# A graph network on one core: the adjacency build on four sets of one-hots, norms with ACT's squares, column sums by DVE, late self loops, and a store in chunks

## The chip, the cores and the metric

The kernel runs on one core of a Trainium2 chip. The metric is device microseconds (us) of one execution. The kernel before was run three times: the median is 2507.62 us, the runs lie between 2501.81 and 2509.18 us.

## What is computed

The reference is a chain of four pre-norm residual layers on a graph of N = 3125 nodes with D = 64 features and E = 103,125 directed edges (50,000 drawn pairs in both directions and one self loop per node), sorted by their target:

```python
h = relu(layernorm(x)); x = x + sage_sum_twice(h)      # L0: agg @ Wl.T + b + h @ Wr.T, row norm between
h = relu(layernorm(x)); x = x + relational(h)          # L1: each edge's message uses one of 16 matrices
h = relu(layernorm(x)); x = x + gat_three_times(h)     # L2: attention over the edges of each target
h = relu(layernorm(x)); x = x + sage_mean_twice(h)     # L3: as below
# sage_mean: agg / max(deg, 1) @ W_neigh.T + h @ W_self.T + b
# after each: leaky_relu((z - mean) * rsqrt(var + eps) * gamma + beta), mean and var over all nodes
```

## The kernel before

**Tiles.** The nodes lie in NT = 25 tiles of P = 125 partitions. The activations (x_sb, l_h, l_z) are 125 x 25 x 64 in fp32, 1600 values a partition. A chunk is TC = 5 tiles, 320 values a partition; there are NC = 5 chunks. The adjacency matrix `adj` lies in SBUF in 16 bits, 25 blocks of 125 rows by 3125 columns and a little padding.

**The build** (L260 to L362) makes `adj` from the edge list. The sorted edges are taken in GB = 202 groups of 512, that is four tiles (GT) of 128 edges. The targets of one group fall in a window of W = 20 columns that starts at a base column, read from `base_row` into a register. For each of the four tiles, DVE writes a one-hot matrix of 500 columns, `col_hot` (L285: block of the source times place in the window). The one-hots of the sources inside a block, `src_hot`, are made by DVE (L288) and by ACT, which makes one or two of the four (`ACT_TILES`) by a square (L306) and a relu (L312). PE multiplies the pairs into a PSUM bank (L349), then adds the window's old content to the same bank by a matmul with the identity (L354), since windows of neighbouring groups overlap; ACT writes the bank back to `adj` (L320). There are two sets of one-hots, two PSUM banks, and each engine's loop has two groups in its body. The waits between the engines are those in this piece of PE's code:

```python
base = pe.value_load(base_row[0:1, bass.ds(g, 1)], min_val=0, max_val=N)   # L344
pe.wait_ge(s_hot, g + 1)        # DVE's one-hots
pe.wait_ge(s_src, g + 1)        # ACT's relus
for t in range(GT): last = pe.matmul(sums, src_hot[...], col_hot[...], ...)  # L349
last.then_inc(s_used, 1)        # DVE may write this set again
pe.wait_ge(s_written, g)        # ACT has written window g - 1
pe.matmul(sums, ident16[...], adj[:, :, bass.ds(base, W)], ...)              # L354
```

The program's loops (`Fori`) are real loops of the chip's sequencers, with a branch at the end of each round; L360 is that of PE's loop. DVE waits for `s_used` of two groups ago.

**Norms.** `layer_norm_relu` runs three times, ahead of l0, l1 and l3, each in a block of its own; it is a chain of whole-width DVE instructions (L400 to L408) with one square root on ACT (L413). The third one, ahead of the last stage, also has POOL subtract the identity from the 25 diagonal blocks of `adj` (L393), which removes the self loops that the attention layers needed. Each block ends in a barrier of all engines.

**Aggregation layers.** `sage_layer` splits h into a high and a low fp16 part (`l_parts`), and PE works chunk by chunk: 50 matmuls of the aggregation (`spmm`, L495), five transposes (L503), then the projections of the chunk before (L514, L515), which DVE reads out of PSUM and turns into z (L451 to L453). In the two layers of the last stage (l3a, l3b), `sums_over_nodes` (L524) adds five fp32 matmuls a chunk with a matrix of ones, which sum z over the nodes.

**Batch norms.** `batch_norm_lrelu` puts the mean together from these sums (L1070 to L1072), subtracts it from all of z (L1073), squares it in five pieces (L1076), sums the squares over the nodes with 25 fp32 matmuls (L1052), and scales, shifts and applies the leaky relu in three DVE instructions of 1600 (L1098 to L1100). After the first of them a bound of h is formed as well. After the second follow `add_residual` (L1624) and `store` (L1633, one DMA of all of x), each in a block of its own.

## Time and profile before

| | |
|---|---|
| median of three runs (lowest to highest) | 2507.62 us (2501.81 to 2509.18) |
| the profiled execution's own time | 2511.9 us |
| its span in the profile | 2509.8 us |
| busy PE, PE's weight loads, DVE, ACT, POOL | 1892.3, 980.2, 1640.6, 1242.8, 1119.8 us |

Busy times are sums over the whole span. By stage, PE's and DVE's shares differ much: the build takes the stretch from 42.5 to 398.4 us, the first layer goes on to 555, the relational layer takes 555 to 1480, the attention layers 1480 to 2289, the last stage the rest. In the rows below PE is TensorE, PEld its weight loads, DVE VectorE, ACT ScalarE, POOL GpSimd, SP SyncE; a q behind an engine marks its sequencer. Each fp32 matmul leaves two records. PEclk is the granted clock of PE as a share of the upper level.

### The profile page before, as it was taken

What the parts mean: (1) busy time and instruction counts of PE and PEld (TensorE: products, weight loads), DVE (VectorE), ACT (ScalarE), POOL (GpSimd) and SP (SyncE); (2) the same over time, 40 slices, a digit from 0 to 9 for tenths busy, and PEclk for the clock granted to TensorE, in tenths of its full rate; (3) what the DMA queues carried; (4) which work ended last, traced back from release to release, by engine and by line L of the source; (5) the groups of instructions that cost most, each with busy time, mean ns of one, the idle gap of its engine ahead of it and who ended that gap; (6) DMA issues with size and microseconds to landing.
All of it is one profiled execution on the core that took longest, in us unless ns stands there. A gap on an engine that the chain in (4) does not pass through costs nothing. (4 is left out here: it accounts for less than half of the span.)

```text
span 2509.8 us, 35723 instructions
## 1 busy us (share of the span) xinstructions
PE 1892.3 (75%) x8956; PEld 980.2 (39%) x8957; DVE 1640.6 (65%) x4139; ACT 1242.8 (50%) x2362; POOL 1119.8 (45%) x1003
## 2 busy tenths in 40 slices
PE   2777776863788878887888865779878876886885
PEld 1333333541344434443443445234423342332654
DVE  8888885223565655665665635998699869984222
ACT  5777773111333333333333320789578957894010
POOL 3000000006666666666666641578467846785000
PEclk9999998876889889898988975899789979998776
DMA  1000001001111111111111112000000000000000
GB/s 61 0 0 0 0 0 63 1 26 36 35 27 30 31 28 32 28 28 32 28 31 29 28 20 88 1 1 1 1 1 0 1 1 1 1 1 13 1 1 13
DMA packets 28313, 44.95 MB, mean 18 GB/s; under 512 B 12381, under 2 KB 12762, under 8 KB 28115
## 3 DMA queue, kind: packets, MB, share of 16 engines
q0 software_dynamic: 17664, 18.12, 4.5%
q1 hardware_dynamic: 10576, 25.91, 2.8%
q8 instruction: 39, 0.64, 0.1%
q14 instruction: 34, 0.28, 0.0%
HBM read 36.60 MB, written 7.39 MB: 18 GB/s over the span
## 5 line engine op out<-in xcount | busy, mean ns | idle before, releaser
L729 POOL DMA_INDIRECT adj<-h_table,l_idx x544 | 561.2, 1032 | 330.4 <-issue 145.8
L919 DVE TENSOR_SCALAR adj<-adj,node_key 125x1024 f16<-125x1024 f16 x825 | 375.5, 498 | 369.0 <-remote 165.7
L1428 POOL TENSOR_TENSOR gat_ring<-gat_ring,adj 125x750 f32<-125x750 f32 (+2 forms) x375 | 503.3, 1342 | 215.3 <-ACT gat_ring L1484 211.0
L864 PE MATMUL psum<-adj,x_sb 125*128 125x512 f16 x1650 | 447.2, 418 | 57.4 <-DVE adj L919 49.2
L792 ACT ACTIVATE l_z<-psum 128x320 f32<-128x320 f32 x204 | 89.3, 438 | 573.9 <-remote 265.3
L1322 DVE SCALAR_TENSOR_TENSOR gat_ring<-x_sb,gat_node,psum 125x750 f32<-125x750 f32 (+2 forms) x375 | 322.0, 867 | 53.1 <-PE psum L1560 41.7
L1482 ACT ACTIVATE gat_ring<-gat_ring,gat_node 125x750 f32<-125x750 f32 (+2 forms) x375 | 304.4, 812 | 63.7 <-DVE gat_ring L1322 60.1
L1557 PE MATMUL psum<-gat_ring,gat_hx 125*65 125x500 f32 (+1 forms) x500 | 253.4, 599 | 68.5 <-POOL gat_ring L1428 67.7
L349 PE MATMUL psum<-col_hot,src_hot 128*125 128x500 bf16 x808 | 209.6, 381 | 113.1 <-ACT src_hot L312 70.3
L1484 ACT ACTIVATE gat_ring<-gat_ring 125x750 f32<-125x750 f32 (+2 forms) x375 | 271.9, 725 | 11.9
L864 PEld LDWEIGHTS psum<-adj,x_sb 125*128 125x128 f16 x1650 | 169.9, 106 | 262.1 <-DVE adj L919 67.7
L285 DVE TENSOR_SCALAR col_hot<-iota_h,c_tab 128x500 bf16<-128x500 f16 x808 | 227.5, 347 | 53.9 <-PE psum L349 53.8
L1291 DVE SCALAR_TENSOR_TENSOR psum<-adj,gat_node,psum 125x750 f32<-125x750 f16 (+1 forms) x276 | 259.8, 941 | 1.3
L676 POOL IOTA l_z<- 128x320 int32 x1 | 0.4, 393 | 545.1 <-issue 545.1
L495 PE MATMUL psum<-adj,l_parts 125*128 125x500 f16 x1000 | 156.7, 322 | 52.3 <-DVE l_parts L442 52.3
L843 PE MATMUL psum<-adj 128*128 128x320 bf16 x816 | 150.1, 307 | 46.8 <-DMA adj<-h_table,l_idx 44.0
L349 PEld LDWEIGHTS psum<-col_hot,src_hot 128*125 128x125 bf16 x808 | 94.9, 137 | 200.6 <-DVE src_hot L288 141.5
L853 PE MATMUL psum<-l_z,l_rel 128*64 128x120 f32 x1088 | 163.1, 286 | 0.0
L1557 PE MATMUL psum<-gat_ring,gat_o 125*65 125x500 f32 (+1 forms) x250 | 129.8, 614 | 31.8 <-POOL gat_ring L1428 31.4
L853 PEld LDWEIGHTS psum<-l_z,l_rel 128*64 128x64 f32 x1088 | 116.2, 143 | 91.9 <-issue 89.5
L907 DVE TENSOR_SCALAR adj<-l_iota,adj 128x320 bf16<-128x320 f16 x612 | 149.4, 299 | 2.6 <-PE psum L843 2.1
L320 ACT ACTIVATE adj<-psum 125x500 f32 x202 | 123.1, 609 | 51.5 <-PE psum L354 46.1
(241 smaller groups left out, 2205.1 us busy)
## 6 DMA issues: line engine op xcount, KB each, us to landing
adj<-h_table,l_idx POOLq DMA_INDIRECT x544
adj<-key_table SPq DMA_DIRECT2D x33, 250.0 KB
adj_saved<-adj SPq DMA_DIRECT2D x1, 3840.3 KB
adj<-adj_saved SPq DMA_DIRECT2D x5, 768.1 KB
x_saved<-x_sb SPq DMA_DIRECT2D x2, 781.2 KB
x_sb<-x_saved SPq DMA_DIRECT2D x2, 781.2 KB
x_sb<-in_x SPq DMA_DIRECT2D x1, 781.2 KB
out<-x_sb SPq DMA_DIRECT2D x1, 781.2 KB
```

The costliest lines, as they stand in the source:

```text
L285: last = v.tensor_scalar(col_hot[:, half, t, :], iota_h[:, :], c_tab[:, bass.ds(g * GT + t, 1)], None, ALU.is_equal)
L349: last = pe.matmul(sums, src_hot[:, half, t, 0:P], col_hot[:, half, t, :], start=(t == 0), stop=False)
L729: pool.indirect_dma_start(out=to[:, t, :], out_offset=None, in_=table[:, :], in_offset=bass.IndirectOffsetOnAxis(ap=index[:, t:t + 1], axi ...
L853: last = pe.matmul(psum[0:D, SUMS[half], 0:SIX * W], rel[:, r, :], zs[:, half, r, :, :].rearrange("p a w -> p (a w)"), start=(r == 0), sto ...
L864: last = pe.matmul(psum[:, 3 + t, :], h_parts[:, k, :], select[0:P, k % SELECTS, t * GE:(t + 1) * GE], start=(k == 0), stop=(k == NT - 1), ...
L919: v.tensor_scalar(select[0:P, k % SELECTS, :], keys, node_key[:, k:k + 1], None, ALU.is_equal).then_inc(s_sel, 1)
L1291: v.scalar_tensor_tensor(to, here, a_unit[:, k:k + 1], so_far, ALU.min, ALU.max).then_inc(s["max_step"], 1)
L1322: v.scalar_tensor_tensor(by_tile(ring[:, n % RING, 0:width(c)]), by_tile(rrow[:, 0:width(c)]), k_s[:, k:k + 1], in_psum(ROW1, c), ALU.add, ...
L1428: pool.tensor_tensor(slot, slot, adj[:, k, cols(c)], ALU.mult).then_inc(s["weight_ready"], 1)
L1482: act.activation(slot, slot, ACT.Relu, scale=-1.0, bias=neg_a_s[:, k:k + 1]).then_inc(s["exponent_bounded"], 1)
L1484: act.activation(slot, slot, ACT.Exp, scale=-1.0).then_inc(s["exp_ready"], 1)
L1557: last = pe.matmul(sums[:, 0:near, 0:P], hx[:, k, :], by_tile(ring[:, n % RING, 0:near * P]), start=(k == 0), stop=(k == NT - 1))
```

## The change

The change touches six places.

1. The build has four sets of one-hots, four PSUM banks and four groups a round, with a remainder of two groups behind the loop. The weights of its matmuls are 128 columns wide instead of 125. ACT writes the window of three groups ago (`AHEAD`), where it was two, and loads that base behind the squares of its step. The table `cv` of the preparation shares the memory of the new sets.
2. The semaphores of the preparation are cleared by SP while the adjacency's tail is spilled, so that their numbers can be used again.
3. In `layer_norm_relu`, the subtraction and the sum go in five chunks, and ACT makes the squares.
4. Of the 25 self loops, POOL removes 15 in the norm and ten inside the next aggregation layer, ahead of the chunks that read them.
5. z's column sums are taken on DVE: a reduce over the five tiles of a chunk. One accumulating set of five matmuls then sums over the partitions and chunks, for the mean; the squares (now ACT's) are reduced and summed in the same way.
6. The last batch norm scales, shifts and applies the relu chunk by chunk; POOL adds each chunk to x, and SP stores it.

```diff
-ACT_TILES = (2, 1)
+ACT_TILES = (2, 1, 2, 1)
+SETS = len(ACT_TILES)
...
+LATE_LOOPS = 10
...
-        src_hot = sb("src_hot", [128, 2, GT, 128], BF16, build_scope)
-        col_hot = sb("col_hot", [128, 2, GT, W * NT], BF16, build_scope)
...
+        src_hot = sb("src_hot", [128, SETS, GT, 128], BF16, build_scope)
+        col_hot = sb("col_hot", [128, SETS, GT, W * NT], BF16, build_scope)
+        cv = col_hot[:, 2:4, :, :].rearrange("p s t w -> p (s t w)").bitcast(FP32)[:, 0:2 * G * GT]\
+            .rearrange("p (k c) -> p k c", k=2)
...
-                    with dve.Fori(1, GB // 2) as i:
-                        for half in range(2):
-                            dve.wait_ge(s_used, 2 * i + half - 1)
-                            one_hots(2 * i + half, half)
+                    for g in range(SETS):
+                        one_hots(g, g)
+                    with dve.Fori(1, GB // SETS) as i:
+                        for at in range(SETS):
+                            dve.wait_ge(s_used, SETS * i + at - SETS + 1)
+                            one_hots(SETS * i + at, at)
...
+                    def step(g, at):
+                        squares(g, at)
+                        base = base_of(g - AHEAD)
+                        write_columns(g - AHEAD, (at - AHEAD) % SETS, base)
+                        act.wait_ge(s_used, g - SETS + 1)
+                        relus(g, at)
...
-                            g = 2 * i + half
-                            base = base_of(g - 2)
-                            act.wait_ge(s_src, g - 1)
-                            one_hots(g, half)
-                            write_window(g - 2, half, base)
-                            relus(g, half)
...
-                        sums = psum[0:P, half, 0:W * NT]
+                        sums = psum[:, at, 0:W * NT]
                         for t in range(GT):
-                            last = pe.matmul(sums, src_hot[:, half, t, 0:P], col_hot[:, half, t, :], start=(t == 0),
-                                             stop=False)
+                            last = pe.matmul(sums, src_hot[:, at, t, :], col_hot[:, at, t, :], start=(t == 0), stop=False)
...
-                    with pe.Fori(1, GB // 2) as i:
-                        group(2 * i, 0)
-                        group(2 * i + 1, 1)
+                    for g in range(SETS):
+                        group(g, g, g == 0)
+                    with pe.Fori(1, GB // SETS) as i:
+                        for at in range(SETS):
+                            group(SETS * i + at, at)
...
-                        with pool.Fori(0, NT) as t:
...
-                            pool.tensor_tensor(own, own, ident[0:P, 0:P], loops).then_inc(s_loops, 1)
...
+                            pool.tensor_tensor(own, own, ident[0:P, 0:P], ALU.subtract).then_inc(s_loops, 1)
...
-                    link(v.tensor_tensor(tmp, x_sb[:, :, :], over_features(stat[:, 0, :]), ALU.subtract))
-                    link(v.tensor_tensor(h, tmp, tmp, ALU.mult))
-                    link(v.tensor_reduce(stat[:, 1, :], h, AX.X, ALU.add))
+                    for tiles in chunks:
+                        v.tensor_tensor(tmp[:, tiles, :], x_sb[:, tiles, :], over_features(stat[:, 0, tiles], TC), ALU.subtract)\
+                            .then_inc(s_centred, 1)
+                    for c, tiles in enumerate(chunks):
+                        dve.wait_ge(s_squared, c + 1)
+                        link(v.tensor_reduce(stat[:, 1, tiles], h[:, tiles, :], AX.X, ALU.add))
...
+                    for c, tiles in enumerate(chunks):
+                        act.wait_ge(s_centred, c + 1)
+                        act.activation(h[:, tiles, :], tmp[:, tiles, :], ACT.Square).then_inc(s_squared, 1)
...
+                        for t in range(NT - loops, NT):
+                            own = adj[:, t, t * P:(t + 1) * P]
+                            pool.tensor_tensor(own, own, ident[0:P, 0:P], ALU.subtract).then_inc(s_less, 1)
...
+                        if column_sums is not None:
+                            dve.wait_ge(s_zc, c + 1)
+                            v.tensor_reduce(column_sums[:, c, :], zc.rearrange("p t d -> p d t"), AX.X, ALU.add).then_inc(s_sums, 1)
...
+                        if loops is not None and (c + 1) * TC > NT - loops:
+                            pe.wait_ge(s_less, (c + 1) * TC - (NT - loops))
...
-                    def sums_over_nodes(c):
-                        pe.wait_ge(s_zc, c + 1)
-                        bank, place = (5, c) if c < 3 else (4, c - 3)
-                        at = TC * D + place * D
-                        for t in range(TC):
-                            pe.matmul(psum[0:P, bank, at:at + D], ones[0:P, 0:P], z[:, c * TC + t, :], start=(t == 0),
-                                      stop=(t == TC - 1))
...
-                        if c >= 2 and column_sums:
-                            sums_over_nodes(c - 2)
...
+                for done in (s_sg, s_key, s_keys, s_nodes, s_dg, s_ti, s_x, s_mats, s_mats2, s_vecs, s_zeroed, s_zeroed2, s_iota,
+                             s_ident, s_ident2, s_chain, s_diag, s_basebc, s_span, s_spanall):
+                    sp.sem_clear(done)
...
-                        for t in range(NT):
-                            if t % TC == 0:
-                                pe.wait_ge(s_sq, t // TC + 1)
-                            last = pe.matmul(psum[0:P, 1, 0:D], ones[0:P, 0:P], h[:, t, :], start=(t == 0), stop=(t == NT - 1))
-                        last.then_inc(s_sumsq, 1)
...
+                        def over_nodes(bank, parts_of, ready, done):
+                            for c in range(NC):
+                                if ready is not None:
+                                    pe.wait_ge(ready, c + 1)
+                                end = pe.matmul(psum[0:P, bank, 0:D], ones[0:P, 0:P], parts_of[:, c, :], start=(c == 0),
+                                                stop=(c == NC - 1))
+                            end.then_inc(done, 1)
+
+                        over_nodes(5, sums, None, s_mean)
+                        over_nodes(1, square_sums, s_sq, s_sumsq)
...
+                        for c, tiles in enumerate(chunks):
+                            act.wait_ge(s_centred, c + 1)
+                            act.activation(h[:, tiles, :], z[:, tiles, :], ACT.Square).then_inc(s_squared, 1)
...
+                        def _(pool):
+                            for c, tiles in enumerate(chunks):
+                                pool.wait_ge(s_final, c + 1)
+                                pool.tensor_tensor(x_sb[:, tiles, :], x_sb[:, tiles, :], h[:, tiles, :], ALU.add).then_inc(s_added, 1)
+
+                        @block.sync
+                        def _(sp):
+                            for c, tiles in enumerate(chunks):
+                                sp.wait_ge(s_added, c + 1)
+                                sp.dma_start(out[:, tiles, :], x_sb[:, tiles, :]).then_inc(s_out[c], 16)
+                            for c in range(NC):
+                                sp.wait_ge(s_out[c], 16)
...
-                        link(v.scalar_tensor_tensor(bn[:, 0, :], bn[:, 1, :], 1.0 / N, bn[:, 0, :], ALU.mult, ALU.add))
-                        link(v.tensor_tensor(z[:, :, :], z[:, :, :], over_tiles(bn[:, 0, :]), ALU.subtract))
-                        for c in range(NC):
-                            tiles = slice(c * TC, (c + 1) * TC)
-                            v.tensor_tensor(h[:, tiles, :], z[:, tiles, :], z[:, tiles, :], ALU.mult).then_inc(s_sq, 1)
...
+                        link(v.tensor_scalar(bn[:, 0, :], psum[0:P, 5, 0:D], 1.0 / N, None, ALU.mult))
+                        for tiles in chunks:
+                            v.tensor_tensor(z[:, tiles, :], z[:, tiles, :], over_tiles(bn[:, 0, :], TC), ALU.subtract)\
+                                .then_inc(s_centred, 1)
+                        for c, tiles in enumerate(chunks):
+                            dve.wait_ge(s_squared, c + 1)
+                            v.tensor_reduce(square_sums[:, c, :], h[:, tiles, :].rearrange("p t d -> p d t"), AX.X, ALU.add)\
+                                .then_inc(s_sq, 1)
...
+                        else:
+                            for c, tiles in enumerate(chunks):
+                                zc = z[:, tiles, :]
+                                v.tensor_tensor(zc, zc, over_tiles(bn[:, 0, :], TC), ALU.mult).then_inc(s_scaled, 1)
+                                dve.wait_ge(s_scaled, c + 1)
+                                v.tensor_tensor(zc, zc, over_tiles(beta, TC), ALU.add).then_inc(s_moved, 1)
+                                dve.wait_ge(s_moved, c + 1)
+                                v.scalar_tensor_tensor(h[:, tiles, :], zc, 0.01, zc, ALU.mult, ALU.max).then_inc(s_final, 1)
...
-            layer_norm_relu("l3", h[:, :, :], z[:, :, :], ALU.subtract)
...
+                       mat("S_self1"), True, column_sums=sums, loops=LATE_LOOPS)
...
-            add_residual(nc, sem("l3_residual"), x_sb, h)
-        store(nc, sem, out, x_sb)
```

On PE, in the body of the build's loop, one group stands like this before, with the branch behind it (the first of the two groups of a round has no branch):

```order
L344 ISA
L344 TENSOR_LOAD base_row
L344 ISA x2
L345 REGISTER_ALU
L349 MATMUL psum<-col_hot,src_hot 125x500 [waits src_hots_ready,col_hots_ready]
L349 MATMUL psum<-col_hot,src_hot 125x500 x3
L354 ISA [waits window_written]
L354 MATMUL psum<-adj,ident 125x500
L360 REGISTER_ALU
L360 COMPARE_AND_BRANCH
```

And so it stands in the changed kernel, where three more groups of the same form are ahead of it in the round:

```order
L358 ISA
L358 TENSOR_LOAD base_row
L358 ISA x2
L359 REGISTER_ALU
L363 MATMUL psum<-col_hot,src_hot 128x500 [waits src_hots_ready,col_hots_ready]
L363 MATMUL psum<-col_hot,src_hot 128x500 x3
L367 ISA [waits window_written]
L367 MATMUL psum<-adj,ident 128x500
L373 REGISTER_ALU
L373 COMPARE_AND_BRANCH
```

The order within a group is the same; the branch comes once in four groups instead of once in two, and the output has 128 partitions.

On ACT, one step of the build's loop (the one with a single square) reads like this before, from the load of the base to the relu:

```order
L316 ISA
L316 TENSOR_LOAD base_row
L316 ISA x2
L306 ISA [waits src_hots_ready]
L306 ACTIVATE square<-iota_h,lo_tab 128x128
L320 ISA [waits outer_done]
L320 ACTIVATE adj<-psum 125x25x20
L311 REGISTER_ALU
L312 ACTIVATE src_hot<-square 128x128 [waits squares_ready]
```

The same step in the changed kernel:

```order
L315 ISA
L315 ACTIVATE square<-iota_h,lo_tab 128x128
L325 ISA
L325 TENSOR_LOAD base_row
L325 ISA x2
L328 REGISTER_ALU
L329 ISA [waits outer_done]
L329 ACTIVATE adj<-psum 125x25x20
L320 REGISTER_ALU [waits hots_used]
L321 ACTIVATE src_hot<-square 128x128 [waits squares_ready]
```

The base's load has moved from ahead of the square to between the square and the window's write, and the relu now waits for PE's use of its set.

On DVE, the end of the program before, from the scaling of the second batch norm on (the barriers between blocks show as branches; names of semaphores behind a program's middle are those of numbers used before):

```order
L1098 TENSOR_TENSOR l_z<-l_z,l_bn 125x1600 [waits l1_gathered2]
L1099 TENSOR_TENSOR l_z<-l_z,vecs 125x1600 [waits l1_gathered2]
L1100 SCALAR_TENSOR_TENSOR l_h<-l_z 125x1600 [waits l1_gathered2]
L1046 UNCONDITIONAL_BRANCH [waits l1_gathered2]
L1622 UNCONDITIONAL_BRANCH [waits barrier_Pool_Activation_PE_DVE_SP_release]
L1624 TENSOR_TENSOR x_sb<-x_sb,l_h 125x1600
```

In the changed kernel, the first chunk and the start of the second:

```order
L1166 TENSOR_TENSOR l_z<-l_z,l_bn 125x320 [waits src_groups_in]
L1168 TENSOR_TENSOR l_z<-l_z,vecs 125x320 [waits l1_picked_turned]
L1170 SCALAR_TENSOR_TENSOR l_h<-l_z 125x320 [waits l1_picked_T_copied]
L1166 TENSOR_TENSOR l_z<-l_z,l_bn 125x320
L1168 TENSOR_TENSOR l_z<-l_z,vecs 125x320 [waits l1_picked_turned]
```

The three wide instructions have become fifteen narrow ones, and the residual add has left DVE.

## Rows read from the trace of the kernel before

**Rows 1.** Windows by stage: the build. Stretch, length, busy (count), PEclk, DMA share, GB/s.

```profile
42.50:398.40 355.90, 259.90 (x1010) 122.37 (x1010) 299.43 (x1308) 273.73 (x700) 0.00 (x0) 1.00 0.00 0
```

**Rows 2.** Timeline inside the build: start, busy us, engine, line, operation, tiles [idle before].

```profile
199.79 0.63 ACT L320 ACTIVATE adj<-psum 125x500 f32 x1 [0.36 <-PE psum L354]
202.23 0.69 ACT L306 ACTIVATE square<-iota_h,lo_tab 128x128 f16<-128x128 f16 x2 [0.35 <-ACT src_hot L312]
203.36 0.63 ACT L320 ACTIVATE adj<-psum 125x500 f32 x1 [0.43 <-PE psum L354]
201.95 1.03 PE L349 MATMUL psum<-col_hot,src_hot 128*125 128x500 bf16 x4 [0.97 <-ACT src_hot L312]
202.82 0.41 PE L354 MATMUL psum<-adj,ident 125*125 x1
203.07 1.01 PE L349 MATMUL psum<-col_hot,src_hot 128*125 128x500 bf16 x4
200.60 0.41 DVE L288 TENSOR_SCALAR src_hot<-iota_neg,lo_tab 128x128 bf16<-128x128 f16 x2
```

**Rows 3.** PE's sequencer at its loop's end: ns min/median/max, first and last start.

```profile
L360 PEldq FUSED_REGOPS  x100: 59/59/64, 45.9 to 394.1; - x100
L360 PEldq COMPARE_BRANCH  x100: 79/211/234, 49.7 to 397.3; - x100
```

**Rows 4.** Groups of instructions, weight loads: busy, mean ns, idle before, releasers.

```profile
L349 PEld LDWEIGHTS psum<-col_hot,src_hot 128*125 128x125 bf16 x808 | 94.9, 137 | 200.6 <-DVE src_hot L288 141.5 <-issue 28.9
...
L843 PEld LDWEIGHTS psum<-adj 128*128 128x128 f16 x816 | 64.4, 99 | 99.3 <-DVE adj L907 44.0 <-issue 38.4
```

**Rows 5.** Timeline of the first norm, its first and last step shown.

```profile
402.96 1.83 DVE L402 TENSOR_TENSOR l_z<-x_sb,stat 125x1600 f32<-125x1600 f32 x1
...
408.53 0.18 DVE L405 TENSOR_SCALAR stat<-stat 125x25 f32<-125x25 f32 x1
```

**Rows 6.** Timeline of the third norm: POOL's self loops and DVE's subtraction.

```profile
2289.43 14.16 POOL L393 TENSOR_TENSOR adj<-adj,ident 125x125 f32 x25 [7.68 <-PEq L375]
...
2291.43 1.97 DVE L402 TENSOR_TENSOR l_z<-x_sb,stat 125x1600 f32<-125x1600 f32 x1
```

**Rows 7.** PE in layer l3a, timeline; the last row is a window's clock.

```profile
2325.66 6.91 PE L495 MATMUL psum<-adj,l_parts 125*128 125x500 f16 x50
...
2332.93 1.21 PE L524 MATMUL psum<-l_z,ones 125*125 125x64 f32 x10
2333.97 0.38 PE L514 MATMUL psum<-mats,l_agg 128*125 128x64 f32 x2
...
2337.53 8.53 PE L495 MATMUL psum<-adj,l_parts 125*128 125x500 f16 x50
...
2366.23 2.36 PE L524 MATMUL psum<-l_z,ones 125*125 125x64 f32 x10 [1.63 <-DVE l_z L453]
...
2337.40:2340.90 3.50, 3.50 (x15) 0.51 0.00 0
```

**Rows 8.** Groups of POOL's instructions by form, in the attention layers.

```profile
L1428 POOL TENSOR_TENSOR gat_ring<-gat_ring,adj 125x375 f32<-125x375 f32 x75 | 65.8, 878 | 108.3 <-ACT gat_ring L1484 107.5
```

**Rows 9.** Timeline of the second batch norm and the end of the program.

```profile
2474.23 0.49 DVE L453 TENSOR_TENSOR l_z<-l_z,vecs 125x320 f32<-125x320 f32 x1
...
2480.50 2.10 DVE L1076 TENSOR_TENSOR l_h<-l_z 125x320 f32<-125x320 f32 x5
2481.04 10.76 PE L1052 MATMUL psum<-l_h,ones 125*125 125x64 f32 x50 [3.91 <-DVE l_h L1076]
...
2493.24 1.82 DVE L1098 TENSOR_TENSOR l_z<-l_z,l_bn 125x1600 f32<-125x1600 f32 x1
...
2499.32 1.82 DVE L1624 TENSOR_TENSOR x_sb<-x_sb,l_h 125x1600 f32<-125x1600 f32 x1 [0.54 <-PEq L1046]
...
2501.62 0.27 SPq L1633 DMA_DIRECT2D out<-x_sb  x1
```

**Rows 10.** DMA over 2480 to 2512 us, in 40 slices of 0.75 us.

```profile
GB/s 0 0 0 0 0 0 0 0 0 0 0 0 0 0 0 0 0 0 0 0 0 0 0 0 0 0 0 16 96 112 136 120 136 128 128 128 0 0 0 0
```

More of the change, by code:

```diff
@@ L342, in _, with group @@
                 def _(pe):
-                    def group(g, half, first=False):
+                    def group(g, at, first=False):
                         base = pe.value_load(base_row[0:1, bass.ds(g, 1)], min_val=0, max_val=N)
@@ L553, in _ @@
                 act.wait_ge(s_wscale, 3)
+        prep_sems.close()
         with ExitStack() as scope:
```

146 lines of the change are left out of this document (81 added, 65 removed).

## Prediction

> **What bounds the kernel now.** I read the table by stage first. The build of the adjacency blocks takes 356 of 2510 us, at the upper clock level (granted clock 1.00), and no engine in it is full: DVE 299, ACT 274, PE 260 us [rows 1]. Then I read a few groups of it in order of time, and asked which wait ends last. A group is four one-hot matmuls, an identity matmul that adds the old window, and ACT's write of the window. The list of waits names DVE's one-hots as what PE waits for. The times deny it: DVE's one-hots for the matmuls at 201.95 were done at 201.01 (200.60 + 0.41). What ends last is PE's own sequencer. A write ends at 200.42 (199.79 + 0.63); only then does PE issue the identity matmul behind it, take the loop's branch, load the next base, and start the next four matmuls at 201.95. Their identity matmul runs at 202.82, its write from 203.36 to 203.99, and the circle of two groups closes: 1.53 + 0.87 + 0.54 + 0.63 = 3.57 us [rows 2]. The whole build gives 355.9 / 101 pairs = 3.52 [rows 1]. So DVE's idle time is a result of this circle, and its sets of one-hots are not what it runs out of.
>
> The rest that the edit touches is the last 220 us and the norms. The norms are a DVE chain [rows 5]. The two batch norms are bound by PE: 25 fp32 matmuls on single tiles, 10.76 us (50 records, each matmul leaves two) at the lower level [rows 9]. The last stage ends with DVE, a residual add, and one store that is issued at 2501.62 and waited for until 2509.8 [rows 9].
>
> **Build: four sets.** A write still releases the next identity matmul, and the base is still loaded behind it, so the circle stays. What shrinks is the number of branches: 100 become 49. Without a branch, PE goes from one group's matmuls to the next's in 203.07 − 201.95 = 1.12 us; with one, the way from the write's end is 1.53, or 0.41 more at most. The branch's instructions alone take 0.211 + 0.059 us and a third small one [rows 3], so at least 0.27. I take 0.36, between the two, since gaps lie between sequencer instructions too: 51 x 0.36 = **18.5 us** (14 to 21). ACT now writes group g−3 behind its squares. ACT is busy 274 / 202 = 1.36 us a group [rows 1], and in the step with two squares (0.69 [rows 2]) a write, its relu and they come to some 1.5; the circle asks for a write each 1.6 on average, so the order costs nothing, or a few us. If ACT lost 0.1 us a group, 20 us would be gone.
>
> Weights of 128 columns instead of 125 load in 99 ns and not 137 [rows 4]. Only the first load of a group's four is bare on the circle, so 101 x 0.04 = 4 us at most, nothing at least; I take 1, as the matmuls of rows 2 already start within the load. The Trainium skill ("TensorE: Matmul & The Clock Gate", Weight-path perf modes) says that fast weight load is on when the weights are 128 and not fp32, and calls it about twice as fast as measured; the trace agrees in sign, with a factor of 1.4. A factor of two would make the term 7 us at most.
>
> Next to the spill DMA, SP clears twenty semaphores. No row of mine has a clear; at a sequencer instruction's 0.06 us [rows 3] that is 1.2 us, behind ACT's work there by half: **−0.8** (0 to −1.5).
>
> **Norms.** Subtract, square and reduce take 5.57 us as three DVE instructions, 402.96 to 408.53 [rows 5]. Now five subtracts at a spacing of 0.40 (five 320-wide ones take 2.10 [rows 9]) are followed by five linked reduces of 0.49 [rows 9] with 0.03 between them (5.57 less three of 1.83 leaves 0.08): 2.0 + 2.7 = 4.7. ACT's squares lie under them: its write of 500 values takes at most 0.63 [rows 2], so five of 320 end by 3.7 and the last reduce starts later. **0.87** each in two norms. The third is longer than its DVE work, because POOL removes 25 self loops, 14.16 us from 2289.43 on [rows 6], and the next stage waits for it until 2303.6. With 15 there, both end near 2299.5: **4.1** (3 to 5). The ten late ones are needed by the fourth chunk, 40 us on; they may hold DVE's first split by 0.3. Sum of this part **5.5**.
>
> **Column sums off PE.** In each of the two last aggregation layers PE has five sums of five fp32 matmuls. Three lie in its full stream at 1.04 to 1.21 us each, the fourth at the lower clock, 2.36 [rows 7]; DVE's reduce that replaces each is 0.49 and lies in DVE's idle time. 3 x 1.08 + 2.1 = 5.3 a layer, **10.6** for both. (The fifth stands in the next part.)
>
> The clock adds to it. After the stretch of fp32 matmuls 2332.93 to 2337.5 the granted clock is 0.51, that is 1.2 GHz, and the next 50 aggregation matmuls take 8.53 us and not the 6.91 of the chunk before, which followed a shorter such stretch [rows 7]. I give back two such drops of the four: 2 x 1.6 = **3.3** (0 to 6.5).
>
> **Batch norms.** I count from the end of the last z. Before, in the second: squares from 5.78 on, their matmuls end at 17.1, the scaling starts at 18.5 [rows 9]. After: reduce 0.52, barrier 0.54, five matmuls 2.36, a small instruction 0.3 (0.18 [rows 5] and the hand-over): subtract from 3.75 on (so the fifth sum's 2.36 is paid as before); five subtracts to 5.85; five reduces at 0.40 to 7.95; one last matmul 0.7 (2.36 / 5 and the hand-over); then the 1.44 from 2491.80 to 2493.24 as before: scaling at 10.1. **8.4**. The first one also forms a bound, in small DVE instructions that 10 us of matmuls covered; with half a microsecond of them bare now, **7.9** (7 to 8.4).
>
> **Last stage's end.** Before, from 2493.24 to 2509.8: 16.5 us [rows 9]. After, DVE does three linked instructions of 0.49 + 0.03 a chunk, the third followed at a spacing of 0.42 by the next chunk's first: 5 x 1.46, 7.4 to the end of the last. POOL's add of a chunk (878 ns for 375 wide [rows 8], so 0.78 for 320) meets DVE. In the trace, DVE's two-input subtract beside POOL takes 1.97 instead of 1.83 [rows 5, 6], and POOL's loops of 125 values average 0.57 us where 375 values cost 0.88. I charge DVE 0.6 for each of four adds, 2.4 (0 to 3.1). Then the last add 0.85, and a store of a fifth of the bytes: of the whole one's 8.2 us, bytes move in nine slices of 0.75, some 6.6 [rows 9, 10], so 1.6 + 6.6 / 5 = 2.9; I take 3.5, as small rows may move slower. Sum 7.4 + 2.4 + 0.85 + 3.5 = 14.2: **2.3** (0 to 4.7).
>
> The Trainium skill ("GPSIMD Engine Reference", Specifications) says that POOL shares its SBUF interfaces with DVE, with contention where DVE has two SBUF inputs; every instruction of DVE's there has. By this rule the adds would give nothing, the worst end of my range, and the trace's 1.97 beside 1.83 agrees in kind.
>
> **Sum.** 18.5 + 1 − 0.8 + 5.5 + 10.6 + 3.3 + 8.4 + 7.9 + 2.3 = 56.7 us. The profiled execution took 2511.9 (span 2509.8 and 2.1 around it), which gives 2455; the median of the runs is 4.3 lower, so I forecast **2451 us**.
>
> **Rivals.**
> 1. *DVE becomes the build's bound* (0.08). If the waits on used one-hots were the cause, four sets would bring the build to DVE's 299 us of work or a little under, a gain of 57 or more instead of 19: 2451 − 38 = 2413. For it: DVE's share of 84% and its wait on PE. Against it: the circle above, which holds with any number of sets, at 3.57 − 0.36 = 3.2 us a pair.
> 2. *The build gains nothing* (0.12): ACT's new order (two squares and a base load ahead of each write) delays writes by the 0.1 us a group. Then 2451 + 19 = 2470.
> 3. *The clock drops stay, and POOL's adds starve or stall DVE* (0.10): 3.3 and 2.3 are lost: 2457. The rule above, alone, costs 2.3: 2453.
> 4. *Slower* (0.02): ACT's steps serialise. The other stages gain 37 us, so the build must lose 37 + 7.5, that is 0.22 us a group over 202 groups, from 1.76 to 1.98. ACT's work is 274 / 202 = 1.36 us a group [rows 1]; only if a base load of some 0.6 us stood bare in each step, behind the squares' end, would it reach that. At 2.1 us a group it gives 2451 + 19 + 69 = 2539. For it: ACT's write is now the instruction behind the load. Against: the load runs on the sequencer while the squares run on the engine, and the edit puts it there.
>
> **How the numbers follow.** My sum has 0.68, the rivals 0.32. Its own range, by the bounds: build 14 to 25, clock 0 to 6.5, end 0 to 4.7, loops 3 to 5, so 2442 to 2462; some us more for how the unchanged stages fall (the runs shown spread over 7 us). Leaving out rivals 1 and 4 and reaching to most of 2: **2438 to 2469**. A measurement of this kernel tells no change from 0.3%, 7.5 us. Faster 0.97, within it 0.01, slower 0.02.
>
> **What would show it.** Build: the pair of groups at 3.3 us on average, writes in two alternating distances, DVE's idle before its first one-hot of a group smaller but not gone; at 2.9 us rival 1 is right, at 3.5 rival 2. The weight loads of the build at 99 ns. Norms: 4.7 us from the first subtract to the variance. Third norm: next stage 4 us sooner. Aggregation layers: no fp32 sums between chunks, 50-matmul chunks at 6.9 us more often than at 8.5. Batch norms: scaling 10.1 us behind the last z in the second, some 12 in the first. End: five adds on POOL, DVE's instructions beside them over 0.49 us, the last store issued 10 to 11 us behind the first scaling. I am wrong if the build's circle is shorter than its pieces (then 2413), or if ACT's write starts later than 0.6 us behind its identity matmul.

## The result, and the profile after

The changed kernel takes 2450.49 us (median of four runs, 2449.44 to 2452.02), the kernel before 2507.96 (2501.81 to 2509.18): a ratio of 0.9774 with a 95% interval of 0.9762 to 0.9786, or 57.5 us less. The prediction was 2451. The profiled execution after took 2449.45 us; against the profiled one of before, 62.4 us are gone, where the sum of the prediction's terms was 56.7. So the forecast hit the median partly by luck; the terms must be read one by one.

The page of the changed kernel, its span and first line of busy times:

```profile
span 2447.7 us, 35160 instructions
PE 1842.0 (75%) x8796; PEld 902.9 (37%) x8797; DVE 1654.5 (68%) x4183; ACT 1236.4 (51%) x2387; POOL 1125.3 (46%) x1008
```

The table by stage, the build (columns as in [rows 1]):

```profile
42.50:374.60 332.10, 253.27 (x1010) 85.54 (x1010) 301.80 (x1308) 256.64 (x697) 0.00 (x0) 1.00 0.00 0
```

The last write of the build ends at 374.55 us and at 398.32 before, and 101 pairs take 3.29 us each where they took 3.52 [rows 1]. In the changed build, in order of time, some rows of DVE, ACT and PE (rows between them are left out at each mark):

```profile
199.99 0.42 DVE L292 TENSOR_SCALAR src_hot<-iota_neg,lo_tab 128x128 bf16<-128x128 f16 x2
...
201.14 0.41 ACT L321 ACTIVATE src_hot<-square 128x256 bf16<-128x256 f16 x1
...
202.38 1.01 PE L363 MATMUL psum<-col_hot,src_hot 128*128 128x500 bf16 x4
...
202.65 0.64 ACT L329 ACTIVATE adj<-psum 125x500 f32 x1 [0.82 <-PE psum L367]
...
203.42 0.39 PE L367 MATMUL psum<-adj,ident 125*128 x1
...
204.10 0.59 ACT L329 ACTIVATE adj<-psum 125x500 f32 x1
...
204.41 1.01 PE L363 MATMUL psum<-col_hot,src_hot 128*128 128x500 bf16 x4 [0.61 <-DVE src_hot L292]
```

The write ends at 203.29, the identity matmul starts at 203.42, and the next four matmuls at 204.41, 0.99 later. Counted through from the loop's start, the matmuls at 204.41 are those of group 98 (the first is group 0). DVE's one-hots for this group are the row at 199.99 and ACT's the row at 201.14: they were complete at 200.41 and 201.55. With four sets DVE is by then at work on the third group after this one, and its one-hots wait some 4 us for PE. The name behind the wait is again DVE's, and again it is PE's sequencer that comes last: it stood at the wait for the write, with the base load behind it. This is the same circle as in [rows 2], now with a branch in every second turn. The turn shown has none (a branch follows groups 95 and 99), so what fills most of its 0.99 us is the load of the base, 0.30 us, and the small instructions behind it. The sequencer's rows for the load and for the branch, which itself is unchanged (ns min/median/max):

```profile
L358 PEldq TENSOR_LOAD <-base_row x202: 296/300/317, 36.0 to 371.6; - x101
...
L373 PEldq COMPARE_BRANCH  x49: 76/208/227, 55.8 to 370.5; - x49
```

The weight loads are shorter, by their group on the page:

```profile
L363 PEld LDWEIGHTS psum<-col_hot,src_hot 128*128 128x128 bf16 x808 | 65.8, 97 | 223.2 <-DVE src_hot L292 171.1
```

The first norm and the third, from the timeline (the counterparts of [rows 5] and [rows 6]), and the start of the layer behind the third:

```profile
380.00 2.10 DVE L420 TENSOR_TENSOR l_z<-x_sb,stat 125x320 f32<-125x320 f32 x5
382.02 2.56 DVE L424 TENSOR_REDUCE stat<-l_h 125x5 f32<-125x320 f32 x5
384.61 0.18 DVE L425 TENSOR_SCALAR stat<-stat 125x25 f32<-125x25 f32 x1
...
2262.72 1.82 DVE L417 TENSOR_REDUCE stat<-x_sb 125x25 f32<-125x1600 f32 x1 [1.00 <-PEq L1249]
2262.86 6.89 POOL L408 TENSOR_TENSOR adj<-adj,ident 125x125 f32 x15 [7.69 <-PEq L390]
...
2264.86 3.12 DVE L420 TENSOR_TENSOR l_z<-x_sb,stat 125x320 f32<-125x320 f32 x5
...
2274.95 2.18 PE L535 MATMUL psum<-adj,l_parts 125*128 125x500 f16 x7 [16.49 <-DVE l_parts L475]
```

In the first norm, 4.61 us lie between the first subtraction and the variance (5.57 before). In the third, the five subtractions take 3.12 us beside POOL and not 2.10, and 12.23 us pass from the norm's first reduce to the next layer's first matmul. The two rows that bound the same stretch before:

```profile
2289.28 1.82 DVE L400 TENSOR_REDUCE stat<-x_sb 125x25 f32<-125x1600 f32 x1 [0.99 <-PEq L1180]
2305.23 9.27 PE L495 MATMUL psum<-adj,l_parts 125*128 125x500 f16 x50 [20.20 <-DVE l_parts L442]
```

That is 15.95 us. PE in the layer l3a after the change, the 50 matmuls of chunks two to five (counterparts of [rows 7]):

```profile
2284.61 6.93 PE L535 MATMUL psum<-adj,l_parts 125*128 125x500 f16 x50
2295.39 6.91 PE L535 MATMUL psum<-adj,l_parts 125*128 125x500 f16 x50
2306.16 6.93 PE L535 MATMUL psum<-adj,l_parts 125*128 125x500 f16 x50
2316.95 8.56 PE L535 MATMUL psum<-adj,l_parts 125*128 125x500 f16 x50
```

One of the two long chunks is short now; in l3b both are (6.93 and 6.91). The granted clock of the fourth and the fifth chunk of l3a, in windows (columns: stretch, length, PE busy (count), PEclk, DMA share, GB/s):

```profile
2306.20:2309.70 3.50, 3.50 (x28) 1.00 0.00 0
2317.00:2320.50 3.50, 3.50 (x16) 0.56 0.00 0
```

The fourth is at the upper level, where it had 0.51 before [rows 7]; the fifth starts at the lower one, behind 3.5 us of fp32 matmuls as the fourth did. The second batch norm and the end of the program (counterparts of [rows 9]):

```profile
2421.47 0.49 DVE L486 TENSOR_TENSOR l_z<-l_z,vecs 125x320 f32<-125x320 f32 x1
2421.99 0.69 DVE L491 TENSOR_REDUCE l_sums<-l_z 125x64 f32<-125x320 f32 x1
2423.28 2.33 PE L1092 MATMUL psum<-l_sums,ones 125*125 125x64 f32 x10 [2.90 <-PEq L452]
...
2427.93 3.10 DVE L1137 TENSOR_REDUCE l_square_sums<-l_h 125x64 f32<-125x320 f32 x5
2428.68 3.08 PE L1092 MATMUL psum<-l_square_sums,ones 125*125 125x64 f32 x10 [3.06 <-DVE l_square_sums L1137]
...
2433.19 0.49 DVE L1166 TENSOR_TENSOR l_z<-l_z,l_bn 125x320 f32<-125x320 f32 x1
2433.72 0.49 DVE L1168 TENSOR_TENSOR l_z<-l_z,vecs 125x320 f32<-125x320 f32 x1
...
2434.81 1.04 POOL L1116 TENSOR_TENSOR x_sb<-x_sb,l_h 125x320 f32<-125x320 f32 x1 [155.97 <-DVE l_h L1170]
2435.17 1.03 DVE L1168 TENSOR_TENSOR l_z<-l_z,vecs 125x320 f32<-125x320 f32 x1
```

From the last z at 2421.96 to the first scaling 11.2 us pass (18.5 before), and 14.5 from there to the end (16.5 before). DVE's shift takes 1.03 where POOL's add runs beside it and 0.49 where it doesn't.

### The profile page after: what moved, and what is told of

It is laid out like the page before. It is cut to its first block and busy times, and to the rows that moved or that the text cites. A ratio compares the mean times of both kernels' runs of the same rounds, so it can differ in the third digit from the quotient of the medians.

```text
span 2447.7 us, 35160 instructions
## 1 busy us (share of the span) xinstructions
PE 1842.0 (75%) x8796; PEld 902.9 (37%) x8797; DVE 1654.5 (68%) x4183; ACT 1236.4 (51%) x2387; POOL 1125.3 (46%) x1008
## 5 line engine op out<-in xcount | busy, mean ns | idle before, releaser
L1626 PE MATMUL psum<-gat_ring,gat_hx 125*65 125x500 f32 (+1 forms) x500 | 258.4, 611 | 66.8 <-POOL gat_ring L1497 66.0
L363 PE MATMUL psum<-col_hot,src_hot 128*128 128x500 bf16 x808 | 205.8, 376 | 97.1 <-DVE src_hot L292 76.5
L885 PEld LDWEIGHTS psum<-l_z,l_rel 128*64 128x64 f32 x1088 | 116.1, 143 | 91.5 <-issue 91.3
L363 PEld LDWEIGHTS psum<-col_hot,src_hot 128*128 128x128 bf16 x808 | 65.8, 97 | 223.2 <-DVE src_hot L292 171.1
```

The lines of the kernel that those rows point to most:

```text
L363: last = pe.matmul(sums, src_hot[:, at, t, :], col_hot[:, at, t, :], start=(t == 0), stop=False)
L885: last = pe.matmul(psum[0:D, SUMS[half], 0:SIX * W], rel[:, r, :], zs[:, half, r, :, :].rearrange("p a w -> p (a w)"), start=(r == 0), sto ...
L1626: last = pe.matmul(sums[:, 0:near, 0:P], hx[:, k, :], by_tile(ring[:, n % RING, 0:near * P]), start=(k == 0), stop=(k == NT - 1))
```

## The experiments

Each ran beside the kernel before on the same chip: runs 5 to 8 on one where that takes 2500.8 us, the others on one where it takes 2348 to 2351, because the relational layer is shorter there (below); the other stages agree within some 3 us. So each time stands beside its own kernel before, and the stages are compared by the traces. "Last write" is the end of ACT's last window write in the build.

**1. Four groups a round, two sets.** The kernel before with the build loops of all three engines unrolled twice (PE's is shown):

```diff
-                    with pe.Fori(1, GB // 2) as i:
-                        group(2 * i, 0)
-                        group(2 * i + 1, 1)
+                    with pe.Fori(0, (GB - 2) // 4) as i:
+                        for k in range(4):
+                            group(4 * i + k + 2, k % 2)
```

> The kernel before, with only the loops of the build changed: four groups in a round instead of two, still on two sets of one-hots, two PSUM banks and weights of 125 columns. If the build is bound by the circle through PE's sequencer (window's write, identity matmul, branch, base load, matmuls), 50 branches fewer give 50 x 0.36 to 50 x 0.47, the price per branch that the build's 23.8 us would mean if branches were all of it: 18 to 23 us, 2485 to 2490 us. If it is the number of sets that gives the change's build its 23.8 us, this kernel gains under 5 us and stays over 2503.

Measured: 2329.05 beside 2348.48, 19.4 us (ratio 0.9919, 0.9905 to 0.9932). The last write ends at 378.83, 19.5 earlier: 0.39 us for each of 50 branches. The rarer branches alone give 19.5 of the build's 23.8 us; the edit takes them from DVE's and ACT's loops too, and no run separates PE's.

**2. Weights of 125 columns.** The changed kernel with `psum[0:P, ...]`, `src_hot[:, at, t, 0:P]` and `ident16[0:P, 0:P]` in PE's group.

> The changed kernel with the build's weights and outputs 125 wide again instead of 128. By the prediction, 1 us is lost (2451.5). If the 4.3 us by which the build gained more than the prediction's sum come from the faster weight loads (137 against 97 ns, bare on each circle of two groups, and the first matmul of a group 396 against 371 ns), 4 to 6 us are lost, 2455 to 2456, and the window writes end 4 to 6 us later.

Measured: 2288.51 beside 2348.48, 60.0 us (ratio 0.9746, 0.9732 to 0.9759); last write at 376.51, 1.96 us later than in the changed kernel. The columns are worth 2.0 us, neither 1 nor 4.3.

**3. The change's build alone**, on the kernel before.

> The kernel before with the build of the changed one (four sets, four groups a round, 128 columns, ACT's new order) and nothing else of the change. The traces of before and after put the end of the build's last write 23.8 us earlier; if that is handed on in full and adds up with the rest, this kernel takes 2483 to 2486 us. If the later stages give some of it back (the clock falls elsewhere), it is nearer 2490.

Measured: 2323.63 beside 2348.48, 24.9 us (ratio 0.9898, 0.9882 to 0.9913); last write at 374.21. The build's gain is handed on in full. 24.9 and the 36.6 that the traces of before and after show for the other edits (the table below, without the stages that were not edited) make 61.5; run 2, on the same chip, has 60.0 with 2.0 undone.

**4. The next base ahead of the wait**, in three of four groups of the changed kernel:

```diff
+                        following = None if then is None else load(then)
                         pe.wait_ge(s_written, g)
```

> The changed kernel, but PE loads the base of the next group behind the four matmuls of a group and ahead of the wait for the window's write, in three of four groups (the first of a round is loaded at its start as before). If PE's sequencer, which stands at that wait with the load behind it, sets the pace, a group falls from 1.64 us to nearly DVE's own 1.48: the build ends 25 to 32 us earlier, and the time is 2419 to 2426. If DVE or ACT sets the pace already with four sets, under 5 us are gained.

Measured: 2267.97 beside 2348.48, 80.5 us (ratio 0.9658, 0.9645 to 0.9671); last write at 356.70, 17.9 us earlier than in the changed kernel. The load's place is what costs. The 17.9 us are under the 25 to 32 expected, since at each branch the load still stands in the circle: the writes' distances in a round are 1.46, 1.25, 1.28 and 2.20 us.

**5. The base behind the matmuls.** Only the identity matmul needs the base, so it is loaded while the group's own four matmuls run:

```diff
-                        base = pe.value_load(base_row[0:1, bass.ds(g, 1)], min_val=0, max_val=N)
                         pe.wait_ge(s_hot, g + 1)
                         pe.wait_ge(s_src, g + 1)
...
                         last.then_inc(s_used, 1)
+                        base = pe.value_load(base_row[0:1, bass.ds(g, 1)], min_val=0, max_val=N)
                         if not first:
                             pe.wait_ge(s_written, g)
```

> The changed kernel, but PE loads a group's base behind its own four matmuls and ahead of its wait for the window's write, where only the identity matmul needs it; in all four groups, those at the branch too. The circle is then write, identity, write: 0.12 + 0.54 + 0.61 = 1.3 us without a branch, and some 2.1 with it, under DVE's 1.46 to 1.48 a group on average. If so, DVE sets the pace and the last write ends at 340 to 348 us (374.6 in the changed kernel, 356.7 with the base ahead), 26 to 34 us faster than the changed kernel. If the load holds the identity matmul back (0.65 us behind the matmuls' dispatch), it ends at 355 to 362.

Measured: 2409.30 beside 2500.81 (ratio 0.9629, 0.9597 to 0.9660), 91.5 us, and 34.1 under the changed kernel in run 7, on the same chip. The last write ends at 334.72, 40.1 us earlier than in run 7 and earlier than any of the expectations. (Some 10 us of them are gone again behind the relational layer, which was 10.6 us longer in this trace than in run 7's; run 12, on the other chip, has them in full.) The table by stage, the build:

```profile
42.50:334.70 292.20, 256.02 (x1010) 83.05 (x1010) 290.29 (x1308) 256.33 (x697) 0.00 (x0) 1.00 0.00 0
```

And DVE and PE of one group in order of time:

```profile
202.66 1.18 DVE L289 TENSOR_SCALAR col_hot<-iota_h,c_tab 128x500 bf16<-128x500 f16 x4
...
203.70 0.46 DVE L292 TENSOR_SCALAR src_hot<-iota_neg,lo_tab 128x128 bf16<-128x128 f16 x2
...
204.29 1.01 PE L362 MATMUL psum<-col_hot,src_hot 128*128 128x500 bf16 x4 [0.17 <-DVE src_hot L292]
```

DVE is busy for 290 of 292 us. Now the wait that names DVE is true: the one-hots of this group end at 204.16 and its matmuls start 0.13 behind. DVE is by then at work on the very next group, where it had been three further on.

**6. The same, with more one-hots by ACT:** `ACT_TILES = (2, 2, 2, 1)`.

> The same as the one with the base behind, and ACT makes two of the four source one-hots in three of four groups instead of two of four: DVE has 0.04 us a group less to do, ACT 0.1 more (1.27 to 1.37). If DVE sets the pace, 202 x 0.04 = 8 us are gained at most, 4 to 8; if the circle or ACT does, nothing or a loss of up to 10 us.

Measured: 2399.67 beside 2500.81 (ratio 0.9592, 0.9561 to 0.9622); last write at 326.34, 8.4 us earlier, just over the 4 to 8 expected. DVE was the bound, and what it is relieved of (202 x 0.04) comes off the time:

```profile
42.50:326.30 283.80, 258.98 (x1010) 84.63 (x1010) 281.90 (x1257) 265.39 (x747) 0.00 (x0) 1.00 0.00 0
```

**7. The changed kernel again.**

> The changed kernel as it is, beside the kernel before on this chip. In the first runs the relational layer took some 165 us less than in the traces of before and after, for all four kernels and for the kernel before alike, while all other stages took the same, so the effect should be the same in microseconds: 57 to 62 us, a ratio of 0.974 to 0.976, and the build's last write ends at 374.5 us again. If the relational layer's waits took part in the change's effect, the difference moves away from that by over 3 us.

Measured: 2443.42 beside 2500.81, 57.4 us (ratio 0.9776, 0.9744 to 0.9809); last write at 374.79.

**8. Column sums on PE as well.** The changed kernel, with `sums_over_nodes(c - 2)` of the kernel before put back for four chunks of each layer, as extra work whose sums nothing reads.

> The changed kernel with additional work: in the two last aggregation layers PE again does the first four of five column sums with five fp32 matmuls each, as before, though nothing uses them. The prediction's terms say 5.3 us a layer for the matmuls; the traces say that three of four clock drops went with them, 1.64 us each. So 10.6 + 4.9 = 15.5 us are lost, and chunks of 50 matmuls that follow a sum take 8.5 us again instead of 6.9. If the clock's drops came from something else, 10.6 are lost and the chunks stay at 6.9; if DVE's reduces were what counts, under 3.

Measured: 2461.15 beside 2500.81 (ratio 0.9834, 0.9797 to 0.9870), 17.7 over run 7. In the traces, l3a and l3b take 70.8 and 71.3 us from the first matmul to the last z, and 64.0 and 62.9 in run 7: 15.3. PE in l3a:

```profile
2292.30 6.91 PE L535 MATMUL psum<-adj,l_parts 125*128 125x500 f16 x50
...
2299.58 1.20 PE L564 MATMUL psum<-l_z,ones 125*125 125x64 f32 x10
...
2304.21 8.48 PE L535 MATMUL psum<-adj,l_parts 125*128 125x500 f16 x50
...
2317.64 8.57 PE L535 MATMUL psum<-adj,l_parts 125*128 125x500 f16 x50
```

With the sums, the drop comes back: the chunks behind the first and the second sum take 8.48 and 8.57 us; l3b has 8.59 and 8.57. In the kernel that this run started from, the second of these is long in l3a too.

**9. The base behind, in the kernel before.** The edit of run 5 and nothing else: two sets, two groups a round, 125 columns.

> The kernel before (two sets, two groups a round, 125 columns), with one edit: PE loads a group's base behind its four matmuls, ahead of the wait for the window's write. If the load's place on PE's sequencer is what held the build, and the sets are of little use, most of the 40 us that this edit gave on the changed kernel come here too: 1.50 to 1.60 us a group instead of 1.755, the last write at 346 to 366 us, 32 to 52 us faster than the kernel before. If four sets are needed for it (DVE waits for the use of its set two groups back, which is 0.87 us of matmuls plus DVE's 1.46 of work in every two groups), 1.65 or more a group and under 22 us.

Measured: 2299.85 beside 2350.65, 50.8 us (ratio 0.9783, 0.9767 to 0.9799); last write at 349.04. One moved line gives in the build twice what the change gives there (49.3 against 23.8), and in all nearly what the whole change gives:

```profile
42.50:349.00 306.50, 273.79 (x1010) 121.50 (x1010) 299.23 (x1308) 266.02 (x700) 0.00 (x0) 1.00 0.00 0
```

The rest of the change's build (four sets, the rarer branch, 128 columns, ACT's order) is worth 14.3 us more once the load is out of the circle (349.0 to 334.7); no run separates these four there.

**10. The residual add on DVE**, chunk by chunk behind the relu.

> The changed kernel, with the last stage's residual add of each chunk on DVE instead of POOL. In the changed kernel a chunk takes DVE 1.99 us, 0.54 of it because the shift runs beside POOL's add (1.03 against 0.49), and the last add on POOL follows 0.08 after with 0.86. On DVE an add costs 0.49 + 0.03 in place of the 0.54: from the first scaling to the end 14.5 now, and 13.6 to 14.6 then; the last store is issued up to 0.8 us earlier. If POOL's contention were more than the 0.54 seen, over 1 us would be gained.

Measured (one run): 2285.66 beside 2350.65. From the first scaling to the end 13.4 us pass, 1.1 less than in the changed kernel and 0.2 less than the 13.6 to 14.6 expected. DVE's shift and add of a chunk:

```profile
2272.79 0.49 DVE L1166 TENSOR_TENSOR l_z<-l_z,vecs 125x320 f32<-125x320 f32 x1
...
2273.84 0.49 DVE L1170 TENSOR_TENSOR x_sb<-x_sb,l_h 125x320 f32<-125x320 f32 x1
```

The shift is back at 0.49, and the add costs DVE as much as POOL's took from it. The last store leaves 0.5 us sooner (10.0 instead of 10.5 behind the first scaling); the other half comes after it and was not traced to a cause.

**11. All self loops in the norm**: `loops=NT` there, none in the aggregation layer.

> The changed kernel, with all 25 self loops removed by POOL inside the third norm, as before, and none in the aggregation layer. The prediction's term says that the stage then waits for POOL again: 25 x 0.46 to 0.57 = 11.5 to 14.2 us from 0.14 behind the norm's start, against 10.4 now until DVE is done; the next layer's first matmul comes 1.5 to 4 us later from the norm's start (12.2 us in the changed kernel). If only the contention with DVE matters, under 1 us.

Measured (one run): 2288.90 beside 2350.65. From the norm's first reduce to the next layer's first matmul 14.0 us pass, 1.8 more than in the changed kernel. The layer behind is 0.7 shorter (63.2 against 63.9) and the one after that 1.2 longer (64.0 against 62.8), because other chunks meet the lower clock: l3a's first and fourth take 8.59 us here (9.29 and 6.93 in the changed kernel) and its fifth 6.91; the granted clock is 0.50 from 2145.00 to 2147.50, in the fourth. So the 0.7 can't be put down to the loops. Norm and layer of this kernel:

```profile
2099.98 1.82 DVE L417 TENSOR_REDUCE stat<-x_sb 125x25 f32<-125x1600 f32 x1 [1.00 <-PEq L1249]
2100.12 12.23 POOL L408 TENSOR_TENSOR adj<-adj,ident 125x125 f32 x25 [7.69 <-PEq L390]
...
2112.88 0.33 DVE L469 TENSOR_SCALAR l_z<-l_h 125x320 f32<-125x320 f32 x1 [1.92 <-PEq L390]
2113.98 4.22 PE L535 MATMUL psum<-adj,l_parts 125*128 125x500 f16 x17 [18.26 <-DVE l_parts L475]
```

POOL needs 12.23 us for its 25 here and needed 14.16 before the change [rows 6], where DVE also made the squares. Single loops show where the 1.93 lie; the first two rows are of the kernel before, the third of this run:

```profile
2291.68 1.99 POOL L393 TENSOR_TENSOR adj<-adj,ident 125x125 f32 x1
2293.63 2.00 POOL L393 TENSOR_TENSOR adj<-adj,ident 125x125 f32 x1
...
2102.99 0.67 POOL L408 TENSOR_TENSOR adj<-adj,ident 125x125 f32 x1
```

A loop takes 0.40 to 0.43 us while DVE reduces. Before, the one that meets DVE's wide subtraction (2291.43, 1.97 long) takes 1.99, and the one that meets its square 2.00. Here five loops meet the five subtractions, at 0.65 to 0.67 each, and there is no square to meet. (A third long one meets the norm's last two-input instruction, 2.00 before and 1.98 here.) So the square's leaving DVE is worth 1.6 of the 1.93, and the subtraction in chunks 0.35.

**12. Three edits together:** runs 5, 6 and 10.

> The changed kernel with three edits together: the base loaded behind the matmuls, two source one-hots by ACT in three of four groups, and the residual add on DVE. Of the changed kernel's time the build's last write came 39.9 us earlier with the first, 8.4 more with the second, and the end was 1.05 shorter with the third. They touch different stages or add up in one, so 49 us under the changed kernel and some 107 to 112 under the kernel before. If the later stages give some of it back, it is under 100.

Measured: 2237.69 beside 2348.46 (ratio 0.9528, 0.9515 to 0.9541), 110.8 us; last write at 326.29, end 13.4. It beats both kernels, and the gains add up.

## Why the prediction came out as it did

The mechanisms named were at work, the total of the third norm had a second cause, and one piece of the build's circle was not weighed. The sizes by the traces are these:

| step | predicted, us | traces, us |
|---|---|---|
| build: branches | 18.5 | 19.5 (run 1) |
| build: 128 columns | 1 | 2.0 (run 2) |
| build: sets and ACT's order | 0 | 2.3 (the rest of 23.8) |
| twenty semaphores cleared | -0.8 | -0.8 (from the last write to the norm's first reduce 2.6, then 3.4) |
| two norms | 1.7 | 1.9 |
| third norm, to the next layer's first matmul | 3.8 | 3.7 |
| column sums off PE | 10.6 | 10.4 |
| clock drops given back | 3.3 | 4.9 |
| batch norms | 7.9 + 8.4 | 7.2 + 7.3 |
| last stage's end | 2.3 | 2.1 |
| all other stages | 0 | 1.7 |
| sum (before rounding) | 56.7 | 62.1 |

**The build.** The circle of write, identity matmul, branch, base load and matmuls held. 0.36 us a branch was 0.39 (and 51 x 0.36 is 18.4, not 18.5). The 128 columns gave 2.0 where 1 was taken, inside the bounds. That four sets bring nothing was not quite right: 2.3 us are left for them and ACT's order together, and which of the two it is stays open. The two rivals on the build fell: it did not become DVE's (run 5 shows how that looks, 290 of 292 us), and no loss by ACT's order shows. One sign that the prediction had named for its being wrong did come: ACT's write starts 0.69 us behind its identity matmul in one of four groups (the row at 204.10 behind the one at 203.42), and 0.50 to 0.54 in the others. It cost nothing, because this write is not on the circle: it ends at 204.69, and the next identity matmul stands behind its own group's matmuls, which start at 204.41 and take 1.01.

**What the prediction missed.** It listed the base load among the circle's pieces and then went on to count branches. Run 9 shows that the load was the larger piece: taken out, it gives 49 us in the build of before, 0.49 a pair of groups, where a branch is 0.39. The statement that the circle "holds with any number of sets, at 3.57 − 0.36 = 3.2 us a pair" is right for this change alone.

**Third norm.** The total was right, its cause only half. The 4.1 us (3.8 with the charge on the first split) were put down to the ten late loops. Run 11 shows 1.8 for them. The other 1.9 come from POOL itself being faster, 12.23 us instead of 14.16 for the same 25 loops: 1.6 because ACT makes the squares and 0.35 because the subtraction is in chunks. The prediction moved the squares to ACT for DVE's sake, counted 0.87 for it in two norms, and did not ask what it does to POOL.

**Layers.** Run 8 puts the sums back and loses 15.3 us in the layers, the 10.4 + 4.9 of the table (4.9 are three times 1.64, a long chunk's 8.56 less 6.92; the medians differ by 17.7, as the relational layer scatters). Three of four clock drops were given back in this trace and not two: in l3a the fifth chunk still takes 8.56 us. Where the drops fall is not fixed: in runs 2, 7 and 12, which have the same layers, l3b's third chunk takes 8.57 and its first one 8.23 to 8.26 instead of 9.83, and the layer is as long (62.8 to 62.9). So what the layers gained is firm, and the count of drops is not. Neither the traces nor a run tell why l3a's last one stays in all of these.

**Batch norms.** The step that was mis-sized is the price of a reduce over the tiles of a chunk. It was taken as 0.49, or a spacing of 0.40; the rows show 0.69 alone and 0.62 a piece in a row of five (3.10 / 5). In the second norm that is 0.2 for the one and 1.1 for the five, against 1.1 that were missing there.

**The end.** DVE's loss beside POOL, taken as 0.6 a chunk, is 0.54. POOL's adds took 1.04 beside DVE and not 0.78, which hides. The Trainium skill ("GPSIMD Engine Reference", Specifications) names the shared interface of POOL and DVE; the trace agrees in that a shift of two SBUF inputs goes from 0.49 to 1.03. By its rule the adds would give nothing, and run 10 bears that out: moved to DVE, they cost no more, and the end is 1.1 shorter.

**The hit on the median.** That the median came out within 1 us of the forecast is luck. The terms were 5.4 us too small in sum. The profiled execution before had been 4.3 above its median and that of after stands 1.0 under its own, and these two together make up for it.

## What to carry to other kernels

When a wait names one engine and its work had ended earlier, look at what the waiting engine's sequencer did in between: an instruction that only its last user needs (here the load of an address) belongs behind the work that doesn't need it, and ahead of the next wait. Ask for every piece of a circle whether it must be in it, before counting how often it occurs; one moved line gave 50.8 us (run 9) where sets, unrolling and wider weights gave 24.9 (run 3). A term that comes out right may have two causes: a run that undoes only one of them tells.

## What the runs showed of the hardware

The relational layer, whose rows are gathered by POOL's indirect DMAs, takes 910 to 925 us in the first measurement and in runs 5 to 8, and some 760 on the chip of the other runs, in all variants alike. (Of the kernel before no trace was kept there; its time is 159 us shorter.) The other stages agree within a few us. The table by stage for the kernel before:

```profile
555.00:1480.00 925.00, 721.69 (x3740) 361.36 (x3740) 531.98 (x1632) 318.59 (x768) 570.80 (x557) 0.87 0.15 30
```

And for run 1:

```profile
536.00:1296.00 760.00, 652.35 (x3766) 345.39 (x3767) 538.98 (x1641) 324.17 (x776) 574.55 (x555) 0.97 0.18 37
```

POOL's busy time is the same (571 and 575 us), PE's granted clock is 0.87 and 0.97. What the stage waits for longer on the slower chip was not settled, nor whether the lower clock is a cause or a result of it. Effects of edits in other stages were nearly the same in microseconds: 57.4 us for the change on a slower chip, 60.0 us with 2.0 of it undone on the fast one.

DVE and POOL hold each other up. Where DVE's wide two-input instruction came first, POOL's loop of 0.42 us took as long as DVE's (1.99 beside 1.97, run 11's paragraph); DVE's shift took 1.03 instead of 0.49 beside POOL's add. A reduce beside POOL's loops took its usual 0.49. DVE also lost time beside POOL in an instruction with one tensor input. The first one of the layer behind the third norm, in the changed kernel, where POOL removes late loops at the same time:

```profile
2273.66 0.60 DVE L469 TENSOR_SCALAR l_z<-l_h 125x320 f32<-125x320 f32 x1 [0.53 <-PEq L390]
```

In run 11, without POOL, it is 0.33. The Trainium skill ("GPSIMD Engine Reference", Specifications) names two kinds of DVE instruction that contend with POOL: those with two SBUF inputs, and those in a 2-port perf mode. The traces agree on the first. This instruction could only be of the second kind; that it is in such a mode no run here shows, but its 0.33 us for 320 values, against 0.49 for a two-input instruction of the same width, would fit.
